# Turning the next block's rows ahead of this block's first products

## The reference, cut to what matters

```python
probs = jax.nn.softmax(flat @ gate_W, axis=-1)
topk_w, topk_idx = jax.lax.top_k(probs, TOP_K)            # two of eight
...
out = 0.5 * jax.nn.gelu(flat @ shared_W + shared_b, approximate=False)
for e in range(n_exp):
    h = jax.nn.gelu(flat @ W1[e] + b1[e], approximate=False)
    out = out + combine[:, e:e + 1] * (h @ W2[e] + b2[e])
```

## Time and profile before

| what | us |
|---|---|
| runs | 725.88, 727.56, 731.08 |
| median | 727.56 |
| profiled execution, span | 729.0 |
| blocks 3 to 35 | about 274.6 to 683 |
| usual length of a block from 17 on | 10.93 |

### The profile page before, as it was taken

One profiled execution on the slowest core, in us unless ns is written; L12 is line 12 of the kernel. 1 busy time (PEld: TensorE's weight loads), 2 busy tenths in 40 slices (PEclk: granted clock), 3 DMA queues, 4 the chain that ended last, 5 costly groups with the idle time before them and its releaser, 6 DMA issues.

```text
span 729.0 us, 16808 instructions
## 1 busy us (share of the span) xinstructions
PE 610.5 (84%) x4903; PEld 517.1 (71%) x4903; DVE 465.5 (64%) x1242; ACT 445.1 (61%) x875; POOL 318.4 (44%) x435
## 2 busy tenths in 40 slices
PE   4778888798876898978979999999999999999600
PEld 3657677677655687866857877889898899888400
DVE  5479898899985554522447776644443544777884
ACT  2657767657744674633654686767567557578742
POOL 4000432535637322654662422245244367574684
PEclk9989999999997899988998999999999999999955
DMA  8553663551255321212111221122211129843466
GB/s 255 181 204 123 197 201 97 192 175 60 95 191 160 92 91 59 60 30 59 46 45 52 90 66 60 32 88 81 75 53 56 41 66 192 173 85 78 84 186 120
DMA packets 45272, 78.25 MB, mean 107 GB/s; under 512 B 16962, under 2 KB 30596, under 8 KB 44804
## 3 DMA queue, kind: packets, MB, share of 16 engines
q1 hardware_dynamic: 33492, 48.19, 20.7%
q0 software_dynamic: 11696, 28.98, 16.8%
HBM read 48.17 MB, written 28.98 MB: 106 GB/s over the span
## 4 chain that ended last, share of the span: by engine, by line
PE 69%; DVE 13%; issue 8%; ACT 4%; POOL 2%; another core or an unknown queue 1%; DMA 1%; DVEq 0%; ACTq 0%; POOLq 0%
PE banks L534 17%; PE banks L536 17%; PE banks L535 16%; PE banks L1022 3%; PE banks L957 3%; PE banks L1192 2%; PE banks L1090 2%; PE banks L980 2%; PE banks L976 2%; DVE W L1747 2%; PE banks L1005 1%; PE banks L1042 1%; DVE st L1601 1%; PE banks L1193 1%
## 5 line engine op out<-in xcount | busy, mean ns | idle before, releaser
L1514 ACT ACTIVATE X<-banks,b1T,tab 128x256 f32<-128x256 f32 x256 | 128.9, 553 | 125.0 <-PE banks L536 98.2
L1980 DVE SCALAR_TENSOR_TENSOR stage<-X,tab,stage 128x512 f16<-128x512 f32 (+1 forms) x160 | 108.7, 697 | 104.0 <-ACT stage L1520 76.3
L534 PE MATMUL banks<-W,stage 128*128 x576 | 160.8, 279 | 10.6 <-issue 7.2
L822 POOL DMA_INDIRECT y_rows<-X,tb x72 | 79.8, 1108 | 202.4 <-DVE X L2011 187.8
L536 PE MATMUL banks<-W,stage 128*128 x576 | 160.6, 279 | 4.3 <-issue 4.3
L535 PE MATMUL banks<-W,stage 128*128 x576 | 160.7, 279 | 2.8 <-issue 2.7
L534 PE MATMUL banks<-X,W 128*128 128x256 f16 x512 | 141.4, 276 | 10.2 <-DVE X L1994 7.9
L536 PE MATMUL banks<-X,W 128*128 128x256 f16 x512 | 141.0, 275 | 0.4 <-issue 0.4
L535 PE MATMUL banks<-X,W 128*128 128x256 f16 x512 | 141.2, 276 | 0.0
L1520 ACT ACTIVATE stage<-X,tab 128x512 f16<-128x512 f32 (+1 forms) x160 | 106.9, 677 | 10.7 <-ACT X L1514 6.9
L797 POOL DMA_INDIRECT table<-pay,slot_i x64 | 67.8, 1059 | 65.8 <-PE banks L1022 42.4
(11 more groups left out here) (300 smaller groups left out, 1155.1 us busy)
## 6 DMA issues: line engine op xcount, KB each, us to landing
stage<-in_L_ffn_W SPq DMA_DIRECT2D x10, 1024.0 KB
W<-in_L_ffn_W SPq DMA_DIRECT2D x6, 1024.0 KB, 8.6
X<-in_L_attn_x SPq DMA_DIRECT2D x8, 512.0 KB, 4.9
out<-X SPq DMA_DIRECT2D x8, 512.0 KB
xf_rows<-zone SPq DMA_DIRECT2D x8, 512.0 KB
u_rows<-b2b SPq DMA_DIRECT2D x8, 512.0 KB
X<-y_rows POOLq DMA_DIRECT2D x8, 512.0 KB
away<-W SPq DMA_DIRECT2D x1, 2048.0 KB, 7.4
```

The lines of the kernel that those rows point to most:

```text
L534: pe.matmul(o, lh, rh, start=first, stop=False)
L822: g.indirect_dma_start(out=y_rows, out_offset=bass.IndirectOffsetOnAxis(ap=tb[:, j % ROWS, h, 1:2], axis=0), in_=y32[:, j % 2 * HALVES + h ...
L1514: a.activation(tile, tile if joint(j) else PS[m][:, r * BT:(r + 1) * BT], ACT.Gelu, bias=b1T[:, bass.ds(e * NH + 2 * m + r, 1)], scale=tab ...
L1980: v.scalar_tensor_tensor(o[1], src, tab[:, 1, bass.ds(e, 1)], o[0], ALU.mult, ALU.subtract).then_inc(h_low, 1)
```

## The change

From block 3 on TensorE runs turn(j + 1) ahead of up(j), no longer between up(j) and down(j - 1). VectorE runs turned_block(j + 1) first in iteration j, no longer between the second and third group of split (or, in joint blocks, ahead of the fourth add_parts). The instructions, semaphores and buffers are the same, and GpSimd's, ScalarE's and SP's lists are untouched.

```diff
@@ -1245,13 +1245,13 @@
             for j in range(3, NB):
+                if j + 1 < NB:
+                    turn(j + 1)
                 up(j, 0, 4)
                 if j == 3:
                     count(B - 2)
                 if j == 6:
                     count(B - 1)
-                if j + 1 < NB:
-                    turn(j + 1)
                 down(j - 1, 0)
@@ -2089,20 +2089,18 @@
             for j in range(3, NB):
+                if j + 1 < NB:
+                    turned_block(j + 1)
                 if joint(j):
                     add_parts(j, 0)
                     add_parts(j, 1)
                     split(j, 0, 1)
                     add_parts(j, 2)
                     split(j, 1, 2)
-                    turned_block(j + 1)
                     add_parts(j, 3)
                     split(j, 2, 4)
                 else:
-                    split(j, 0, 2)
-                    if j + 1 < NB:
-                        turned_block(j + 1)
-                    split(j, 2, 4)
+                    split(j, 0, 4)
```

## The result

The changed kernel takes 742.76 us (median of 4 runs, 738.58 to 746.1) where the kernel before, run beside it, takes 727.5: a ratio of 1.021 (95% interval 1.017 to 1.026), 15 us slower. Its profiled execution has a span of 741.0 us, 12.0 more than that of before. Forecast were 746 us and slower.

What follows compares the result with a forecast made beforehand. TensorE, busy 84% of the span, was taken as the bound, with at most 1.53 us of wait to win directly. 2.5 + 2.7 + 3.1 + 2.7 + 0.5 + 5.6 + 1.4 = +18.5 us gave 747.5, as a median 746; range 732 to 754.

Steps and rivals of the forecast that it cites:

- Block 4, the gain: Ahead of block 4, the first product no longer waits for VectorE's copy of its rows: -1.53 us.
- Block 5: Block 6's transposes, now ahead of block 5's products, wait for their gather: TensorE idles 4.0 us, block 6 starts +2.5 us late.
- The clock: After long TensorE waits in blocks 5, 12 and 31, products run at half clock: +2.7 us each.
- Block 12: Block 13's transposes wait for a gather issued 0.67 us after block 12's first product: +3.1 us, and +2.7 us of clock.
- Blocks 13 to 16: In two-expert blocks the copy delays the first partial sum; 0.24 us each in blocks 13 and 14: +0.5 us.
- Blocks 17 to 30: Gather issues end 2.25 us ahead of the block, for 2.2 to 2.4 us of landing: no wait of size.
- cover of 2.25 us: In blocks 17 to 30, the time from the end of a gather's issue to the block's start, within which rows must land.
- Rival (b): Regular blocks 17 to 30: landing at 3.3 us makes 7 blocks wait 1.05 us, +7.4, 753.5; chance 0.15.
- Block 31: Block 32's gather lands behind accumulating loads: transposes wait 4.8 us, plus 2.7 us of clock; +5.6 us net.
- Tail: From block 32 on, the copy ahead of split is no longer hidden: 2 x 0.69 = +1.4 us for blocks 33 and 34.
- Rival (c): Blocks 6, 7 and 10: the stuck copy feeds TensorE's starving; moving it gains 5.0 us each, -15; chance 0.13, half of it faster.
- my 2.4: The landing time in us assumed between a gather's last issue and its rows being there, in blocks 5 and 12.

Runs made afterwards that it cites:

- before_again: The kernel before, unchanged, run once more for a trace beside the experiments: ratio 1.0004.
- after_again: The changed kernel, unedited, run once more under the experiments' conditions: 708.26 us, ratio 1.0239 to the kernel before.
- e5: Changed kernel with VectorE's copy back in its old place, TensorE's new order kept: 702.72 us, ratio 1.0160 to the kernel before.
- e6: Changed order in block 12 alone, plus 56 useless transposes before TensorE waits for the gather: ratio 1.0046 to the kernel before.
- e8: Kernel before with gathers ahead of scatters on GpSimd (except at j = 9) and the changed order in blocks 32 to 34 alone: ratio 0.9976.
- e9: Kernel before with only gathers ahead of scatters on GpSimd (except at j = 9): 690.18 us, ratio 0.9973.
- e1: Changed kernel with the old order kept in blocks 5, 12, 18, 30, 31 and 33: ratio 1.0081 to the kernel before.
- e2: Kernel before with the changed order in block 3 alone: ratio 0.9996.

## Why the prediction was right, and where it wasn't

The mechanism and the places were right: idle time ahead of L1090, ended by the gather, in blocks 5, 12 and 31. Its sum, step by step, beside the lengths of the same blocks in both pairs of traces (before and after as first profiled; before_again and after_again):

| part | forecast | first pair | second pair |
|---|---|---|---|
| blocks 3 to 5 | +5.2 | +3.8 | +4.5 |
| blocks 6 to 10 | 0 | -0.5 | +0.1 |
| blocks 11 and 12 | +5.8 | +5.5 | +5.8 |
| blocks 13 to 16 | +0.5 | -0.3 | -0.6 |
| blocks 17 to 28 | 0 | +1.5 | +1.9 |
| blocks 29 to 34 | +5.6 | +6.7 | +6.5 |
| block 35 to the end | +1.4 | -2.1 | -3.5 |
| up to block 3 (untouched) | 0 | -2.7 | -1.8 |
| sum | +18.5 | +12.0 | +12.8 |

The profiled execution of before_again was its longest run (695.4 us, median 692.57), and the first one's span of 729.0 lies above its median too, so these sums are smaller than the 15 to 16 us of the medians. Beside the traces the forecast's 18.5 us are half as much again, and single parts are off in both directions; that the median came within 3.2 us of 746 is in part luck.

- **Block 4, the gain.** Right on the first pair: the wait of 1.53 us is gone. Under the other conditions there was none to win.
- **Block 5.** Size within 1.4 us. The wait was 4.03 us as forecast (4.0), by two errors that cancel: a landing of 1.96 us in place of 2.4, and an issue that ends 2.07 us behind TensorE's place (296.10 against 294.03) in place of 1.63. What had been left out is that the result stands behind split too: the copy's 0.66 us reach the gather (e5).
- **The clock.** The step "27 products ran at half speed, some 2.7 us lost" was mis-sized. e6 shows the mechanism; the price in blocks 5 and 12 is 1.66 us each. Behind block 33's wait of 3.13 us it is 0.98 us (block 33 lasts 11.91), as its transposes were already slow (1.03 us). That the clock holds after a wait as short as block 4's 1.53 us was no safe rule either, as the last section shows.
- **Block 12.** The sum was right by two errors that cancel: a wait of 4.11 for 3.1, a clock of 1.66 for 2.7. "Both hang on the end of block 10 and keep their distance" failed: the gather's issue ended 0.67 us behind TensorE's place before, and 2.2 us (402.26 against the products' end at 400.03) after.
- **Blocks 13 to 16.** The step "0.69 - 0.45 = 0.24 us in each of the two blocks" failed: the third group of products waited 0.45 and 0.37 us in blocks 13 and 14, as before (0.46 and 0.37), and the four blocks together became shorter by 0.3 us in the first pair and 0.6 in the second.
- **Blocks 17 to 30.** The cover of 2.25 us held in all blocks but 18 and 30. In block 18 the gather stands behind the result of a two-expert block, which with the copy ahead comes 0.4 us later (2.33 us behind the start of block 17 in after_again, 1.89 in e5), and a 512 KB load on SP's queue goes at the same time: landing 3.34 us, wait 1.59 (1.63 in the second pair). Rival (b), a loop of waits, didn't come.
- **Block 31.** That the gather lands behind the accumulating loads was right: the rows came 1.05 us behind the last of them. The wait of 4.8 us was spread, 0.68, 1.44 and 3.13 us ahead of blocks 30, 31 and 33; in after_again it was nearer to the forecast, 3.76 us ahead of block 31, with half clock behind it. That a late TensorE makes results, scatters and so the next loads late would explain the spread, and is argued.
- **Tail.** Wrong in sign: +1.4 forecast, -2.1 and -3.5 measured. The copy ahead of split costs nothing that shows there; the likely reason is that TensorE comes late and VectorE and ScalarE have meanwhile caught up with the norms. That the order of itself gives nothing there is shown by e8 beside e9; the catching up is argued, and not tried by itself.
- **Rival (c)**, that the stuck copy feeds the starving, is refuted: the copy's waits on "remote" are all gone and blocks 6 to 10 take 78.3 us for 78.7. The Trainium skill's rule (SBUF — State Buffer, Who interferes with whom), by which the copy that reads PSUM doesn't contend with GpSimd, was called at odds with the trace too soon: the waits of up to 7.7 us end on "remote", which names no engine, and in before_again the same copy beside the same GpSimd chain never waits, as the rule has it. So the stuck copy is a companion of the starving, not its cause; what held it isn't shown.

The landing was 1.81 to 2.01 us in the quiet places (ahead of blocks 5, 12 and 13 in all runs), 3.3 to 4.8 beside other traffic. The Trainium skill (DMA: Bandwidth & Descriptors, Anatomy of one DMA) gives some 2.0 us as fixed cost, which the quiet places agree with; with what the same section adds for bytes, an estimate of 0.3 us for the 128 KB of a gather's second half, it would be 2.3, near my 2.4.

## What to carry to other kernels

Before a step is moved ahead, compare the time of its input's last issue, plus its landing (here two microseconds at best), with the new place, in every iteration, and expect the next iteration to be the late one once the first is mended. If it doesn't fit, move the producer first: putting gathers ahead of scatters took 1.7 of the 2.4% back at no cost, and alone made the kernel 0.27% faster. And a wait of TensorE of some 3 us has half clock behind it as part of its price, here 1.2 to 2.5 us, which useless transposes in the wait took away.

## What the runs showed of the hardware

- The same kernel takes 727.5 or 692.3 us: in the first case TensorE stands idle on "issue" again and again while GpSimd issues its writes to the table (block 10 18.59 against 10.93 us), in the other it doesn't, though the same writes are issued. What holds TensorE in the first case isn't shown. Two versions must run beside each other to be compared.
- Behind each of the twelve waits of TensorE for a gather of 2.66 us and more, in all runs, the granted clock fell to 0.50 for a time. The block behind lost 1.66 or 1.67 us in six cases, whether the wait was 2.66 or 4.30 us. In the six others the transposes ran slowly too (1.03 or 1.04 us for 0.62) and the block lost 0.9 to 2.1 us, which with the transposes makes 1.2 to 2.5. More waiting did not cost more clock.
- Below 2 us it went either way: the clock held behind waits of 1.63, 1.73 and 1.96 us (block 5 of e5), and fell behind the 1.96 us ahead of block 32 in e1. It even fell in the unchanged kernel, behind 1.57 us ahead of block 13's third group of products (before_again, block 13 at 0.89 on average), where e2 with the same wait kept 1.00. So there the length of the wait alone doesn't decide.
